# Re-staging the work between attention and the experts of a sandwich block (LayerNorm, projection, router) on one core

## The reference, cut to what matters

```python
x = x + _layernorm(attn(_layernorm(x)))          # x: (2, 1024, 128), 16 heads of 8, causal
x = x + _layernorm(moe(_layernorm(x)))
# attn: scores = q k^T * SCALE (causal -inf) + head_scales * (q.dir)(k.dir);
#       softmax; out = attn @ v; return out @ w_out
# moe:  logits = x_flat @ router_w.T             # 7 experts, top 2
#       combine = one_hot(top_idx) * softmax(top_vals)
#       mixed = sum over e of combine_e * swiglu_e(x) + swiglu_shared(x)
# swiglu: (silu(x @ wg) * (x @ wu)) @ wd, hidden 512; _layernorm: (x - mean) / sqrt(var + 1e-5)
```

## Time and profile before

| what | us |
|---|---|
| median of 3 runs (lowest to highest) | 480.75 (479.73 to 484.54) |
| the profiled execution | 477.46 |
| its span, first to last instruction | 475.7 |
| PE, DVE, ACT, POOL busy in the span | 413.5, 322.9, 259.4, 175.1 |
| first block, up to | 278.6 |
| shared expert and routing, up to the first expert tile | 341.0 |
| expert tiles, up to | 446.0 |

### The profile page before, as it was taken

How to read it: one execution, slowest core, us unless ns; L and a number is a source line. 1 busy time by engine, 2 the same in 40 slices (tenths; PEclk the granted TensorE clock), 3 DMA queues, 4 the chain that set the end, 5 groups by cost and what they waited for, 6 DMA issues and landing times. The chain is left out here.

```text
span 475.7 us, 10729 instructions
## 1 busy us (share of the span) xinstructions
PE 413.5 (87%) x3820; PEld 240.9 (51%) x3820; DVE 322.9 (68%) x1116; ACT 259.4 (55%) x465; POOL 175.1 (37%) x325
## 2 busy tenths in 40 slices
PE   1846899889999999999999878988999999999870
PEld 0521224223233233233343263655799999999870
DVE  2977869979999999999865928498333333333242
ACT  1530458347887887887986628552334443444223
POOL 5000135303123123114263425333766767673302
PEclk9995569869999999999999979999999999999986
DMA  4076112440021122000000044100687788877142
GB/s 116 1 222 177 34 39 78 125 121 16 1 70 37 35 69 65 6 2 4 4 2 3 1 129 137 44 2 1 188 242 240 229 238 234 243 239 233 36 167 88
DMA packets 39031, 46.57 MB, mean 98 GB/s; under 512 B 5635, under 2 KB 26500, under 8 KB 38980
## 3 DMA queue, kind: packets, MB, share of 16 engines
q1 hardware_dynamic: 34820, 39.34, 27.9%
q0 software_dynamic: 2432, 4.99, 3.7%
q10 hardware_dynamic: 1728, 1.57, 1.1%
HBM read 34.80 MB, written 10.88 MB: 96 GB/s over the span
## 5 line engine op out<-in xcount | busy, mean ns | idle before, releaser
L712 ACT ACTIVATE probs<-banks 128x1024 f32<-128x1024 f32 (+1 forms) x192 | 153.0, 812 | 47.6 <-PE banks L553 29.8
L539 PE MATMUL banks<-k_st,q_st 48*128 48x512 bf16 (+3 forms) x384 | 111.9, 358 | 16.4 <-DMA k_st<-k_rows 8.8
L831 DVE CUSTOM_DVE_ANT_0 masked<-banks,mask_max 128x512 bf16<-128x512 f32 (+3 forms) x256 | 110.5, 487 | 17.3 <-PE banks L539 15.9
L553 PE MATMUL banks<-q_st,k_st 51*128 51x512 bf16 (+3 forms) x384 | 100.8, 344 | 4.6 <-DMA q_st<-mx_rows 2.7
L581 PE MATMUL banks<-probs,v_ones 128*9 128x128 f32 (+3 forms) x1536 | 97.7, 340 | 0.6 <-POOL probs L447 0.5
L539 PEld LDWEIGHTS banks<-k_st,q_st 48*128 48x128 bf16 x384 | 31.8, 95 | 101.2 <-DVE mx_part L834 32.3
L834 DVE TENSOR_REDUCE mx_part<-banks 128x1 f32<-128x512 f32 x128 | 77.8, 682 | 3.6 <-PE banks L539 3.3
L447 POOL TENSOR_SCALAR_AFFINE_SELECT probs<-probs 128x256 f32<-128x256 f32 x128 | 52.4, 415 | 64.4 <-ACT probs L712 31.9
L1615 DVE TENSOR_TENSOR hidden<-banks,gate 128x512 f32<-128x512 f32 x38 | 26.3, 692 | 66.4 <-PE banks L1253 64.9
L433 POOL CAST mx_split<-mx 128x16 bf16<-128x16 f32 x16 | 3.1, 196 | 125.9 <-DVE mx L837 75.8
L1128 POOL DMA_INDIRECT results<-result,target x38 | 37.4, 983 | 30.4 <-DVE result L1623 30.4
(11 more groups left out here) (197 smaller groups left out, 473.1 us busy)
## 6 DMA issues: line engine op xcount, KB each, us to landing
w_g<-in_w_gate SPq DMA_DIRECT2D x38, 256.0 KB, 3.3
w_u<-in_w_up SPq DMA_DIRECT2D x38, 256.0 KB, 4.4
q_st<-q_rows SPq DMA_DIRECT2D x32, 96.0 KB, 2.3
k_st<-k_rows SPq DMA_DIRECT2D x32, 96.0 KB, 2.3
q_rows<-parts SPq DMA_DIRECT2D x18, 128.0 KB, 2.4
k_rows<-parts SPq DMA_DIRECT2D x18, 128.0 KB, 2.4
w_d<-in_w_down SPq DMA_DIRECT2D x8, 256.0 KB, 4.5
back<-results SPq DMA_DIRECT2D x4, 512.0 KB, 5.8
```

The lines of the kernel that those rows point to most:

```text
L539: nc.tensor.matmul(max_bank[e % RING][:, 0:width], q_st[g][rows, c, p, (i % CH) * P:(i % CH + 1) * P], k_st[g][rows, kc, p, 0:width], star ...
L553: last = nc.tensor.matmul(dst[a][:, 0:BANK - first], k_st[g][rows, j // CH, p, (j % CH) * P:(j % CH + 1) * P], q_st[g][rows, c, p, first:B ...
L712: last = nc.scalar.activation(probs[s % PROBS][:, 2 * p:2 * p + 2, first:BANK], slot_pair[at % 2].rearrange("p (a t) -> p a t", a=2)[:, :, ...
L831: nc.vector.tensor_tensor_reduce(masked[e % RING][:, 0:width], src, mask_max[:, BANK - width:], 1.0, NEG, ALU.add, ALU.max, accum_out=dst) ...
```

## The change

Batch 0 is transposed after s = 84, projected after s = 85 and 86, and its tokens are transposed after s = 93 and 94; its router matmuls and logits go to the second block. Newton rounds become 3, and batch 1's roots are also made by Newton on DVE. The projection is read by DVE in PSUM (banks 6 and 5), with no copy: x_sb becomes x_sb + projection * rstd, and the missing shift `lag` = -mean * rstd is added during the expert tiles. PE waits for `x2_ready` before shared_down(0), which writes bank 6. Batch 0's top 8 are found early. The exponential of the gap goes to expert tile 2. The one-hots are bf16 throughout, stored with the slot index last.

```diff
-NEWTON = 4
+NEWTON = 3
...
-                if s == item_end(NG * NC + NG) + 1:
+                if s == SCORES_ALONE:
                     first_turn_attn()
-                if s == item_end(NG * NC + NG) + 3:
-                    first_project()
+                if s is not None and 0 <= s - SCORES_ALONE - 1 < 2:
+                    first_project(s - SCORES_ALONE - 1)
+                if s is not None and 0 <= s - SCORES_ALONE - 9 < 2:
+                    first_turn_tokens(s - SCORES_ALONE - 9)
...
-            first_turn_tokens()
-            first_route()
...
+            statistics(first_proj, first_projected)
+            nc.vector.scalar_tensor_tensor(lag[:, 0:KT], mean_var[:, 0:KT, 0], -1.0, rstd[:, 0:KT],
+                                           ALU.mult, ALU.mult).then_inc(vector_steps, step.one())
             for t in range(KT):
...
+                nc.vector.scalar_tensor_tensor(x_sb[:, t, :], first_proj(t), rstd[:, t:t + 1], x_sb[:, t, :],
+                                               ALU.mult, ALU.add).then_inc(vector_steps, step.one())
...
-            nc.vector.tensor_tensor(x_sb[:, 0:KT, :], x_sb[:, 0:KT, :],
-                                    xn_stage[:, :, :, :].rearrange("p h j c -> p (h j) c"), ALU.add
...
-            for k in range(inverted, len(ITEMS) - 1):
-                invert_sums(k)
+            invert_sums(inverted)
...
+            for k in range(inverted + 1, len(ITEMS)):
+                invert_sums(k)
...
-        row_hot = sb("row_hot", [P, 2 * NT, P], BF16)
-        tile_hot = sb("tile_hot", [P, 2 * NT, 3, TILES], BF16)
+        slot_part_b = sb("slot_part_b", [P, 2, 2 * NT], BF16)
+        iota_row = sb("iota_row", [P, P, 2 * NT], BF16)
+        iota_tile = sb("iota_tile", [P, TILES, 2 * NT], BF16)
+        row_hot = sb("row_hot", [P, P, 2 * NT], BF16)
+        tile_hot = sb("tile_hot", [P, 3, TILES, 2 * NT], BF16)
...
-            at_bank, pr_bank = [bank(0), bank(1)], [bank(2), bank(3)]
+            at_bank, pr_bank = [bank(0), bank(1)], [bank(6), bank(5)]
...
+                route(0)
+                route(1)
                 for half in range(2):
                     pe.wait_ge(attn_t_ready, half + 1)
...
                 pe.wait_ge(shared_loaded, 16 * 3)
-                pe.wait_ge(proj_ready, 2)
                 shared_up(0, range(HT))
                 shared_up(1, [0])
+                pe.wait_ge(x2_ready, QC + 1)
                 shared_down(0)
...
-                    last = nc.tensor.matmul(t_out, row_hot[:, k, :],
-                                            tile_hot[:, k, :, :].rearrange("p v a -> p (v a)"),
+                    last = nc.tensor.matmul(t_out, row_hot[:, :, k],
+                                            tile_hot[:, :, :, k].rearrange("p v a -> p (v a)"),
...
-                for half in range(2):
-                    act.wait_ge(projected, half + 1)
-                    nc.scalar.activation(proj[:, half * CH:(half + 1) * CH, :].rearrange("p t c -> p (t c)"),
-                                         pr_bank[half], ACT.Copy).then_inc(proj_ready, 1)
-
-                def standard_deviations(n, at, count):
...
-                act.wait_ge(gap_ready, 1)
-                nc.scalar.activation(gap_exp[:, :], gap[:, :], ACT.Exp).then_inc(gap_exp_ready, 1)
...
+                    if k == 2:
+                        act.wait_ge(gap_ready, 1)
+                        nc.scalar.activation(gap_exp[:, :], gap[:, :], ACT.Exp).then_inc(gap_exp_ready, 1)
+                    if 0 <= k - 5 < 2 * NT:
+                        make_diagonal(k - 5)
...
+                dve.wait_ge(logits_done, QC)
+                nc.vector.tensor_copy(logits[:, 0:KT, 0:E],
...
+                for t in range(KT):
+                    nc.vector.max(top[:, t, :], logits[:, t, :]).then_inc(steps, step.one())
+                done()
+                for t in range(KT):
+                    nc.vector.max_index(top_at[:, t, :], top[:, t, :], logits[:, t, :]).then_inc(steps, step.one())
+                for half in range(2):
+                    dve.wait_ge(projected, half + 1)
+                    statistics(proj, KT + half * CH, CH)
+                inverse_roots(KT, KT)
...
+                    nc.vector.scalar_tensor_tensor(x_sb[:, t, :], proj(t), rstd[:, t:t + 1], x_sb[:, t, :],
+                                                   ALU.mult, ALU.add).then_inc(steps, step.one())
+                done()
+                statistics(lambda t: x_sb[:, t, :], KT, KT)
+                inverse_roots(KT, KT)
...
+                nc.vector.tensor_tensor(
+                    tile_hot[:, 2, :, :], iota_tile[:, :, :],
+                    slot_part_b[:, 0, :].unsqueeze(1).broadcast_to([P, TILES, 2 * NT]), ALU.is_equal
...
+                        row_hot[:, :, part], iota_row[:, :, part],
+                        slot_part_b[:, 1, part].unsqueeze(1).broadcast_to([P, P, NT]), ALU.is_equal
+                    ).then_inc(hot_ready, 1)
...
+                def finish_residual(k):
+
+                    t = k - 8
+                    nc.vector.tensor_scalar(x_sb[:, t, :], x_sb[:, t, :], lag[:, t:t + 1], None, ALU.add
+                                            ).then_inc(residual_ready, 1)
```

More of the change, by code:

```diff
@@ L64 @@
 LOADS = 4
+ROUTE_CONSTS = 10
 class Count:
@@ L844, in _ @@
             dve.wait_ge(consts_ready, 1 + 3)
+            nc.vector.memset(logits[:, :, E:8], NEG).then_inc(vector_steps, step.one())
             inverted = 0
@@ L1428, in layer_norm @@
                     done()
-                    nc.vector.tensor_scalar(var_eps[:, part], mean_var[:, part, 1], EPS, None, ALU.add
-                                            ).then_inc(var_sem, 1)
-                    dve.wait_ge(std_sem, n)
-                    nc.vector.reciprocal(rstd[:, part], std[:, part]).then_inc(steps, step.one())
+                    v, y, e = var_eps[:, part], rstd[:, part], std[:, part]
+                    nc.vector.tensor_scalar(v, mean_var[:, part, 1], EPS, None, ALU.add).then_inc(steps, step.one())
@@ new lines, in inverse_roots @@
+                    for _ in range(NEWTON):
+                        done()
+                        nc.vector.scalar_tensor_tensor(e, y, -0.5, y, ALU.mult, ALU.mult).then_inc(steps, step.one())
+                        done()
+                        nc.vector.tensor_tensor(e, e, v, ALU.mult).then_inc(steps, step.one())
+                        done()
+                        nc.vector.scalar_tensor_tensor(y, e, 1.5, y, ALU.add, ALU.mult).then_inc(steps, step.one())
+                    done()
@@ new lines, in _ @@
+                done()
+                for t in range(KT):
[4 more added lines that the diff above has]
+                inverse_roots(KT, KT)
+                nc.vector.scalar_tensor_tensor(lag[:, KT:], mean_var[:, KT:, 0], -1.0, rstd[:, KT:],
+                                               ALU.mult, ALU.mult).then_inc(steps, step.one())
@@ L1442, in _ @@
                 done()
-                nc.vector.tensor_tensor(x_sb[:, KT:, :], x_sb[:, KT:, :], proj[:, :, :], ALU.add
-                                        ).then_inc(steps, step.one())
-                done()
-                layer_norm(lambda t: x_sb[:, t, :], KT, KT, post_var_ready, post_std_ready, 2)
+                statistics(lambda t: x_sb[:, t, :], KT, KT)
+                inverse_roots(KT, KT)
                 for t in range(KT, NT):
@@ L1451, in _, with pick_experts @@
                         last.then_inc(x2_ready, 1)
-                dve.wait_ge(logits_done, QC)
+                nc.vector.tensor_copy(top_at_f[:, 0:KT, :], top_at[:, 0:KT, 0:2]).then_inc(steps, step.one())
+                dve.wait_ge(route_consts, ROUTE_CONSTS)
+                done()
+                def pick_experts(at, count):
+                    part = slice(at, at + count)
+                    for i in range(2):
+                        nc.vector.tensor_tensor(
+                            pick[i][:, :, part], iota[:, 0:E].unsqueeze(2).broadcast_to([P, E, count]),
+                            top_at_f[:, part, i].unsqueeze(1).broadcast_to([P, E, count]), ALU.is_equal
+                        ).then_inc(steps, step.one())
+                pick_experts(0, KT)
+                dve.wait_ge(logits_done, 2 * QC)
                 nc.vector.tensor_copy(logits[:, KT:, 0:E],
```

207 lines of the change are left out of this document (91 added, 116 removed).

## The result

| | median us | runs, lowest to highest | against before (95%) |
|---|---|---|---|
| before | 480.75 | 5, 478.80 to 484.54 | |
| after | 493.14 | 5, 486.93 to 497.32 | 1.018 (1.011 to 1.025) |

What follows compares the result with a forecast made beforehand. Bound: PE's waits and half clock in the 62.4 us between first block and expert tiles. T -1.2, shared_down(0) 8.45 later against T, -0.8 `picked` wait, +2.0 clock, -1.0, +0.5: 8.0 us over 480.75, 488.7; range 480.5 to 494.

Steps and rivals of the forecast that it cites:

- first rival: Second block: batch 1's roots on DVE are not blocked by POOL's products; 4.9 us less, 483.9 us; chance 0.20.
- second rival: Table matmuls: operands with 64 bytes between elements are slow, +5.4 us instead of +0.5, 493.6 us; chance 0.10.
- T: First PE instruction of the second block, 278.69 before; forecast 1.2 us earlier, at 277.5 (bounds -1.6 and +0.4).
- The blocked roots: Second block: four to five POOL products hold up DVE's 12 root steps, from T + 9.9 to T + 17.2.
- steps that stay at 0.2: Sign against the forecast: Newton steps in the second block stay at 0.2 us instead of some taking over a us.
- The wait as the lever: Before shared_down(0): PE idles some ten us for x2, which moves shared_down(0) from 296.34 to 303.6.
- R: Start of the rank matmuls, 311.05 before; forecast 8.45 us later, at 319.5.
- The clock behind the wait: From shared_down(0) to R: the idle time costs PE its clock, +2.0 us (bounds 0 and 3.5).
- R to the tables: From R to the table matmuls: ACT's exponential table load gone, one-hots still meeting products; -1.0 us (bounds -3.1 and 0).
- The strided operand: Table matmuls, 1.66 us before: operands 64 bytes apart from element to element; +0.5 us (bounds 0 and +5.4).
- What was costed at nothing: POOL's two new iota, and the exponential, weights, `lag` adds and later diagonals under PE in the expert tiles: no cost.
- third rival: Whole change: not slower, since PE has full clock at T and the roots run unhindered; -4.3 us, 476.4 us; chance 0.15.

Runs made afterwards that it cites:

- e4: Kernel after with batch 0's token transposes moved back behind the attention's last outputs; 488.68 us, ratio to before 1.019.
- e8: Kernel after with POOL's shared-expert products held until x2's third quarter is ready; 486.52 us, one run.
- e3: Kernel after with batch 1's projection in another bank, so shared_down(0) no longer waits for x2; 481.81 us, ratio to before 0.995.
- e10: As e6, but eight passes of the table of tiles interleaved, 16 bytes between a pass's values; 480.33 us, ratio to before 0.997.
- e2: Kernel after with only row_hot, the stationary operand, contiguous again; 487.22 us, ratio to before 1.015, 32 passes 6.19 us.
- e12: As e6, but four passes of the table of tiles interleaved, 8 bytes between a pass's values; 474.64 us, ratio to before 0.984.
- e5: Kernel after with both one-hot tables contiguous, no x2 wait before shared_down(0), and batch 0's token transposes late; 475.35 us, ratio to before 0.981.
- e6: As e5, but only tile_hot, the moving operand, contiguous and row_hot still strided; 474.56 us, ratio to before 0.975.
- e9: As e6, but two passes of the table of tiles interleaved, 4 bytes between a pass's values; 469.56 us, ratio to before 0.980.
- e11: The same kernel as e9, measured once more; 471.51 us, ratio to before 0.977.

## Why the prediction was right, and which of its terms were not

Direction and size came out as forecast: 488.7, where the measured ratio makes 489.5 of 480.75. From s = 84 on, 10.0 us were lost where 8.0 were forecast. The main mechanism was the named one: PE waits before shared_down(0) for x2, which DVE now makes alone. That the size fits as well is luck. Most of the first rival came true (the blocking cost 2.5 us and not 4.9, and shared_down(0) came 4.2 us earlier after T than in the sum) and all of the second (the strided operand, 4.4 us too little), and the two errors cancelled.

- **T, -1.2 forecast, +0.1 measured.** x2's first half came earlier than I had it, 21.5 us after s = 84, but PE stood before the transposes sooner still, and waited 2.69 instead of 1.7 us (my terms for T add up to 277.0, not 277.1). From the transposes to T took 11.3 instead of 8.7: the clock fell behind the wait (0.71), for which I had allowed 0.4. e4 puts a number on the whole step: without it T would have come 4.4 us earlier.
- **The blocked roots, T + 9.9 to 17.2 forecast, T + 8.7 to 12.1 measured.** This step failed most. I let four to five products block the 12 steps; one did, and two more hit the lag and the second variance. The first product could start only at T + 10.4, behind a projection at half clock, and by then eight of the 12 steps were over and the ninth had begun. Of the 18 Newton steps one took over a us (1.12) and the others 0.17, so my own sign against the forecast, steps that stay at 0.2, came near. e8 gives the price of all blocking: 2.5 us, not 4.9. The start before that was earlier by 1.2: transposes and router were through 3.5 us after T and not 5.4, and four of the eight statistics ran beside the projection. So shared_down(0) came at T + 21.9 and not at T + 26.1. That is close to where my first rival put it (4.9 earlier), for a part of its reason: DVE was ahead of the products.
- **The wait as the lever.** The forecast had shared_down(0) and all behind it hanging on x2; PE stood 5.42 us there, and not ten. e3 shows it: without that one wait R is 10.3 us earlier. The same x2 is needed two steps later in PE's order, and there nobody waits in e3 (PE waits 2.3 us there in e10).
- **The clock behind the wait, +2.0 forecast.** shared_down(0) lost 1.8 (5.62 against 3.84), and a second stretch from 317 on (granted clock 0.52 up to 320.4, behind 5 us at 1.00 with PE busy for 4.70 of them), which I did not have, took 1.6 more in four matmuls: 3.3 from shared_down(0) to R, without the wait for `picked`. Why the clock falls there is open. My 72% set a chain time (3.53) against a timeline time (2.05); by the timeline alone the 16 passes take 3.68 against 2.05, 80% more, which moves no term by more than 0.3.
- **R to the tables, -1.0 forecast, -2.6 measured.** Of my bounds (-3.1 to 0) the lower was nearer: the last product ended 11.7 after R, and the last three products took 1.42 to 1.55 us instead of 1.27 beside DVE's one-hots.
- **The strided operand, +0.5 forecast, +4.9 measured.** I stood near the row of the contiguous passes and should have stood at the other bound: the second rival's mechanism occurred (its +5.4 was 0.5 too much), and e2 and e10 to e12 show it. No row of the trace could have priced it; the two ends were there, and the choice was wrong. Behind the passes another 0.7 went to the clock, up to the first expert tile.
- **What was costed at nothing** held: POOL's new iota (4.17 and 1.33 us) ended long before the first product, and the expert stage and the tail differ by 0.3 us.

The third rival (not slower, 476.4) was wrong as a forecast, but e5, e6 and e9 reach that side: the parts of the change that remain in e9 and e11, one kernel, are worth 9.7 and 6.6 us from s = 84 on.

## What to carry to other kernels

Put a wait where its data are used, not where a shared buffer forces it: moving a result to another bank took away 8.4 to 10.3 us that looked like the price of a slower chain. A wait of PE can cost itself and then again in clock (2.69 us of wait and 4.4 us of loss in the steps before T), so a transpose squeezed into an earlier step can lose more than it saves if its input is not there yet. Before an operand's layout is changed for the engine that writes it, look at how PE's moving operand reads it: keep at least four bf16 values of a pass within 16 bytes; interleaving two passes gave both engines their quick rate.

## What had not been expected of the hardware

- A moving bf16 operand costs PE 1.8 ns for each 16 bytes touched: 207 ns a pass of 114 columns from 16 bytes of stride on, 109 at 8, 64 at 4. A stationary operand with 64 bytes of stride loads in 144 to 154 ns instead of 98, and a pass still takes 62 (52 with both operands contiguous).
- PE that is busy all the time with such passes still loses part of its clock: 0.93 of full during them, 0.70 in the 4 us behind (e10), where contiguous passes keep 1.00 (e5).
- One and the same kernel varies by 3 us between s = 84 and the first expert tile (85.12 and 88.20), by where the clock falls. The stretch ahead of s = 84, the same work in all kernels here, varies by 10 us.
